# One tile of gathered rows in 64 moves from GpSimd's indirect transfers to 128 single transfers of SP

## What is computed

```python
src, dst = (edge_index[0], edge_index[1])
s_e = s[src]                      # gathered scalars, 8 of the 32 numbers of a row
v_e = v[src]                      # gathered vectors, 24 of the 32
...
out0 = jax.ops.segment_sum(m0, dst, num_segments=n)
out1 = jax.ops.segment_sum(m1.reshape(e, MUL * 3), dst, num_segments=n).reshape(n, MUL, 3)
```

## Time and profile before

| | |
|---|---|
| Median of 3 runs | 4191.23 us (4188.38 to 4191.39) |
| The profiled execution | 4180.82 us, span of its instructions 4179.0 us |
| Busy share | PE 86%, PEld 52%, DVE 79%, ACT 53%, POOL 72% |
| Layer 0, first to last gather | from 26.4 to 2036.7 us |
| Layer 1, first to last gather | from 2100.2 to 4108.0 us |

### The profile page before, as it was taken

How to read it: one execution, slowest core, us unless ns; L and a number is a source line. 1 busy time by engine, 2 the same in 40 slices (tenths; PEclk the granted TensorE clock), 3 DMA queues, 4 the chain that set the end, 5 groups by cost and what they waited for, 6 DMA issues and landing times.

```text
span 4179.0 us, 79599 instructions
## 1 busy us (share of the span) xinstructions
PE 3584.4 (86%) x24746; PEld 2173.1 (52%) x24746; DVE 3311.0 (79%) x5246; ACT 2201.5 (53%) x6573; POOL 3017.6 (72%) x3143
## 2 busy tenths in 40 slices
PE   5888888888888888888649999999999999999995
PEld 3555555555555555555425555555555555555553
DVE  7777777777777777777749988888888889888887
ACT  3555555555555555555325555555555556555553
POOL 5777777777777777777367777777777777777772
PEclk8999999999999999999879999999999999999998
DMA  3111111111111111111132212121212212121212
GB/s 103 33 29 33 29 33 29 34 33 29 33 29 33 29 33 29 33 31 31 18 48 47 46 39 47 37 47 37 47 37 47 47 37 48 37 47 37 47 37 32
DMA packets 220966, 159.83 MB, mean 38 GB/s; under 512 B 125489, under 2 KB 194994, under 8 KB 220466
## 3 DMA queue, kind: packets, MB, share of 16 engines
q0 software_dynamic: 100352, 51.58, 8.8%
q1 hardware_dynamic: 84946, 90.16, 8.2%
q10 hardware_dynamic: 35650, 17.88, 1.6%
HBM read 148.94 MB, written 10.43 MB: 38 GB/s over the span
## 4 chain that ended last, share of the span: by engine, by line
POOL 58%; issue 25%; PE 7%; DVE 6%; DMA 3%; DVEq 1%; POOLq 0%; ACT 0%; SPq 0%; ACTq 0%
POOL rows L364 58%; PE red L687 4%; PE wps L674 2%; DMA rows<-x_rows,src 2%; DVE prod L984 1%; DVE q L1036 1%; DMA src<-in_src 1%; PE wps L667 1%; DVE t_a L1022 0%; DVEq L1064 0%; DVE table L1060 0%; POOLq L381 0%; DMA x_rows<-table 0%; PE acc L701 0%; DMA rows<-in_x,src 0%
## 5 line engine op out<-in xcount | busy, mean ns | idle before, releaser
L364 POOL DMA_INDIRECT rows<-x_rows,src x1568 | 1504.6, 960 | 567.2 <-issue 562.7
L364 POOL DMA_INDIRECT rows<-in_x,src x1568 | 1512.1, 964 | 507.9 <-issue 498.5
L687 PE MATMUL red<-prod,ident 128*128 128x336 f32 (+2 forms) x6272 | 1753.6, 436 | 0.0
L687 PEld LDWEIGHTS red<-prod,ident 128*128 128x128 f32 x6272 | 1145.9, 193 | 651.1 <-issue 189.5
L493 ACT ACTIVATE gap<-iota,slot_plan 128x128 bf16<-128x128 f32 x3136 | 943.7, 387 | 85.3 <-DVE t_b L1087 76.0
L984 DVE TENSOR_TENSOR prod<-wps,q 128x896 f32<-128x896 f32 x784 | 836.3, 1084 | 191.2 <-PE wps L674 175.9
L667 PE MATMUL wps<-bias_parts,ones 64*128 64x448 bf16 (+1 forms) x2352 | 463.6, 391 | 517.4 <-DVE prod L978 324.4
L674 PE MATMUL wps<-w_sb,hidden 64*128 64x256 f32 (+1 forms) x4704 | 903.8, 487 | 0.0
L511 ACT ACTIVATE sums<-red 128x336 f32<-128x336 f32 (+2 forms) x392 | 168.6, 430 | 1084.1 <-PE red L687 1083.1
L667 PEld LDWEIGHTS wps<-bias_parts,ones 64*128 64x128 bf16 x2352 | 114.5, 94 | 1039.6 <-DVE prod L978 422.1
L674 PEld LDWEIGHTS wps<-w_sb,hidden 64*128 64x128 f32 x4704 | 487.5, 204 | 70.4 <-issue 25.6
(11 more groups left out here) (125 smaller groups left out, 3117.4 us busy)
## 6 DMA issues: line engine op xcount, KB each, us to landing
mlp<-in_dist SPq DMA_DIRECT2D x196, 256.0 KB
mlp<-in_feat SPq DMA_DIRECT2D x98, 256.0 KB
rows<-in_x,src POOLq DMA_INDIRECT x1568
rows<-x_rows,src POOLq DMA_INDIRECT x1568
frames<-frame ACTq DMA_DIRECT2D x49, 144.0 KB
geo<-frames ACTq DMA_DIRECT2D x98, 72.0 KB
src<-in_src SPq DMA_DIRECT2D x196, 8.0 KB, 1.6
geo<-in_sh ACTq DMA_DIRECT2D x98, 32.0 KB, 1.7
```

Source lines behind the costliest of these rows:

```text
L364: nc.gpsimd.indirect_dma_start(out=rows[z][:, t, :], out_offset=None, in_=table_rows, in_offset=bass.IndirectOffsetOnAxis(ap=src_sb[z][:, ...
L687: ins = nc.tensor.matmul(red[:, bank * 512:bank * 512 + cols], ident[:], pr[:, i, :, a:b, :], start=(i == 0), stop=(i == MUL - 1))
```

## The change

Every fourth chunk has its last tile (tile 15) fetched by SP instead of POOL. Four chunks make one pass of a new loop on SP and on POOL (`FETCHES` = 24 passes), and the last two of the 98 chunks are done as before. In one pass SP

- loads the 128 indices of that tile into one partition, `fetch_index`;
- loads for each of the four chunks `src` and the network's input, in this order chunk by chunk, and after each fetches 32 rows: eight times it loads four indices into registers, and for each it issues a transfer of one row of the table into one partition of `fetched`;
- waits for all 128 rows, then for the buffer's old rows to be read, and stores `fetched` into tile 15 of `rows[1]` with one transfer from SBUF to SBUF;
- waits until that has landed (`tile_moved`) and turns.

POOL gathers 63 tiles in a pass and adds the missing 16 to `rows_gathered` with `inc_swdge_sem`. DVE and ACT wait for `tile_moved` too before they read the second buffer.

```diff
+FETCH_CHUNKS = 4
+FETCH_ROUNDS = FETCH_CHUNKS // RING
+FETCHES = ROUNDS // FETCH_ROUNDS
+FETCH_ROWS = P // FETCH_CHUNKS
...
+            def fetch_rows(n, part):
+
+                table_rows = x if n == 0 else x1
+                for p in range(part * FETCH_ROWS, (part + 1) * FETCH_ROWS, 4):
+                    _, indices = nc.values_load_multi_w_load_instructions(
+                        fetch_index[0:1, p:p + 4], engines=(mybir.EngineType.SP,), min_val=0, max_val=N_NODES - 1,
+                        skip_runtime_bounds_check_because="the indices of the edges' sources are rows of the table")
+                    for a, index in enumerate(indices):
+                        sp.dma_start(fetched[p + a:p + a + 1, :], table_rows[bass.ds(index, 1), :]
+                                     ).then_inc(row_fetched, 16)
...
+                    with sp.Fori(0, FETCHES) as h:
+                        f = sp.snap(j * FETCHES + h + 1 + n * (count * FETCHES))
+                        sp.dma_start(fetch_index[:], src_fetched[bass.ds(h, 1), :]).then_inc(indices_loaded, 16)
+                        sp.sem_inc(s.tile_moved, 16)
+                        for m in range(FETCH_CHUNKS):
+                            z = m % RING
+                            r = round_of(sp, j, h * FETCH_ROUNDS + m // RING)
+                            k = h * FETCH_CHUNKS + m
+                            load_source(n, z, r, k)
+                            load_mlp(n, z, r, k)
+                            if m == 0:
+                                sp.wait_ge(indices_loaded, f * 16)
+                                if n == 1:
+                                    sp.wait_ge(x1_stored, 16)
+                                sp.sem_inc(fetch_turns, 1)
+                            fetch_rows(n, m)
+                        sp.wait_ge(row_fetched, 16 * P)
+                        sp.sem_clear(row_fetched)
+                        sp.wait_ge(s.rows_read[RING - 1], r)
+                        sp.wait_ge(s.rows_copied[RING - 1], r)
+                        sp.dma_start(rows[RING - 1][:, TILES - 1, :], fetched[:]).then_inc(s.tile_moved, 16)
+                        sp.wait_ge(s.tile_moved, r * 16)
+                        sp.sem_inc(fetch_turns, 1)
+                    sp.sem_inc(s.tile_moved, 16)
+                    for z in range(RING):
+                        r = round_of(sp, j, ROUNDS - 1)
+                        load_source(n, z, r, (ROUNDS - 1) * RING + z)
+                        load_mlp(n, z, r, (ROUNDS - 1) * RING + z)
...
-                for t in range(TILES):
+                for t in range(tiles):
...
+                if tiles < TILES:
+                    pool.inc_swdge_sem([s.rows_gathered[z]], [(TILES - tiles) * 16], mode="add")
...
                 act.wait_ge(s.rows_gathered[z], i * (16 * TILES) + 16 * TILES)
+                if z == RING - 1:
+                    act.wait_ge(s.tile_moved, r * 16)
...
                 dve.wait_ge(s.rows_gathered[z], i * (16 * TILES) + 16 * TILES)
+                if z == RING - 1:
+                    dve.wait_ge(s.tile_moved, r * 16)
```

More of the change, by code:

```diff
@@ L85, in build @@
 def build(nc, x, x_nodes, x_self, src, dst, dst_rows, sh, feat, rel, dist, identity, w1_0, b1_0, w2_0, si, w1_1, b1_1,
-          w2_1, out):
+          w2_1, src_fetched, out):
     x1 = nc.dram_tensor("x1_rows", [BLOCKS * P, FEAT], F32).ap()
@@ L140, in build @@
         span = sb("span", [P, 4])
+        fetch_index = sb("fetch_index", [1, P], I32)
+        fetched = sb("fetched", [P, FEAT])
         span_max = sb("span_max", [P, 2])
@@ L201, in build @@
         windows_moved = sem("windows_moved")
+        indices_loaded = sem("indices_loaded")
+        row_fetched = sem("row_fetched")
+        fetch_turns = sem("fetch_turns")
         class LayerSemaphores:
@@ L219, in __init__ @@
                 self.counts_reset = sem(f"l{n}_counts_reset")
+                self.tile_moved = sem(f"l{n}_tile_moved")
                 self.rows_read = ring("rows_read")
@@ L307, in _, with load_source, load_mlp @@
             sp.dma_start(rel_sb[:], rel).then_inc(loaded["rel"], 16)
+            def load_source(n, z, r, k):
+                s = layers[n]
+                sp.wait_ge(s.rows_read[z], r)
+                sp.dma_start(src_sb[z][:], src[bass.ds(k, 1)].rearrange("k p t -> p (k t)")
+                             ).then_inc(s.src_loaded[z], 16)
+            def load_mlp(n, z, r, k):
+                s = layers[n]
+                if n == 0:
+                    sp.wait_ge(s.hidden_summed[z], r * 2)
+                    sp.dma_start(mlp_sb[z][:, 0:SET], feat[bass.ds(k, 1)].rearrange("k p c -> p (k c)")
+                                 ).then_inc(s.mlp_loaded[z], 16)
+                else:
+                    sp.wait_ge(s.hidden_ready[z], r * 2)
+                    for a in range(2):
+                        sp.dma_start(mlp_sb[z][a * HID:(a + 1) * HID, :],
+                                     dist[bass.ds(k, 1), a, :].broadcast_to([HID, CHUNK // 2])
+                                     ).then_inc(s.mlp_loaded[z], 16)
+            def fetch_rows(n, part):
[7 more added lines that the diff above has]
+                                     ).then_inc(row_fetched, 16)
             def stream(n, count):
@@ L311, in stream @@
                 with sp.Fori(0, count) as j:
[L312 to L329, removed]
@@ L353, in _, with gather @@
                                            bass.bass_isa.ReduceOp.max).then_inc(spans_known, 1)
-            def gather(n, z, r):
+            def gather(n, z, r, tiles=TILES):
                 s = layers[n]
@@ L380, in gather_all @@
                 with pool.Fori(0, count) as j:
[L381 to L384, removed]
+                    with pool.Fori(0, FETCHES) as h:
+                        for m in range(FETCH_CHUNKS):
+                            gather(n, m % RING, round_of(pool, j, h * FETCH_ROUNDS + m // RING),
+                                   TILES - (1 if m == FETCH_CHUNKS - 1 else 0))
+                    for z in range(RING):
+                        gather(n, z, round_of(pool, j, ROUNDS - 1))
                     reset_counts(n, round_of(pool, j, ROUNDS - 1))
@@ L1328 @@
         "src": by_partition(padded(src, EDGES, 0)),
+        "src_fetched": padded(src, EDGES, 0).reshape(CHUNKS, TILES, P)[FETCH_CHUNKS - 1:FETCHES * FETCH_CHUNKS:FETCH_CHUNKS,
+                                                                       TILES - 1],
         "dst": all_by_partition(dst_p),
```

## The result

The changed kernel takes **4403.49 us** in the median of 4 runs (4399.19 to 4409.05), the kernel before on the same chip 4191.31 (4188.38 to 4195.27). The ratio is 1.0506, with an interval of 1.0492 to 1.0521: slower by 5.1%. The prediction was 4390 us.

A forecast was written before the change was run, and what follows sets the result against it. POOL's gathers were taken to bound the kernel before, at 82.0 and 81.8 us for four chunks. SP's summed passes of 84.6 and 87.5 us add 199 us, giving a median of 4390 us, range 4140 to 4750.

The forecast's parts named there:

- The bound: SP becomes the slowest, at 84.6 and 87.5 us a pass against POOL's 82.0 and 81.8 before: +199 us.
- The single transfer: SP's one-row fetch: 0.485 us from one to the next, 128 a pass, 62.1 us; bounds 0.47 and 0.68.
- rival 1: POOL stays the bound and the removed gathers count: SP's pass at 81.0 us, kernel 4142 us, chance 0.15.
- The register load: SP's load of four indices: 0.30 us plus 0.075 for gaps, 32 a pass, 12.0 us; bounds 0.29 and 0.47.
- rival 2: SP's small terms at upper bounds, a register load at 0.47 us: kernel 4650 us, up to 4750, chance 0.17.
- The code: SP's longer loop may fetch its code anew each turn: 2.0 us a pass taken, 0 and 5.6 kept.
- The ends of a pass: SP's waits: 1.3 us for the last row, 1.7 for the store into `rows`, 0.3 for semaphores.
- Rival 3: SP's single transfers are dear, at 0.492 us each: kernel 5590 us, or over twice the time if serial; chance 0.13.

The follow-up runs named there:

- e1: The changed kernel without SP's single-row transfers and register loads, tile 15 of every fourth chunk filled with zeros: 4094.42 us, 0.9778 of the kernel before.
- e3: The changed kernel with sixteen indices in one register load instead of four, 8 loads a pass instead of 32: 4095.95 us, 0.978 of the kernel before.
- e8: The changed kernel with register loads of sixteen indices and the back-branch prefetch hint on SP's loop together: 4096.22 us, 0.9792 of the kernel before.
- e4: The changed kernel with a prefetch hint for the back branch of SP's loop: 4246.39 us, 1.0139 of the kernel before.
- e12: The changed kernel with two indices in one register load instead of four, on another chip: 8022.11 us against 6875.8 for the kernel before.

## Why the prediction was right

**The bound.** Predicted: SP becomes the slowest at 84.6 us a pass in layer 0 and 87.5 in layer 1. Measured: 84.87 and 89.49. The difference between the layers is 4.6 us instead of 2.9. The sum of 24 x (84.87 - 82.0) + 24 x (89.49 - 81.8) is 253 us, against the predicted 199. The profiled execution was longer than that of before by 228 us, and the medians lie 212 apart. Some 8 us of the gap between them are the first index load of layer 1, which lasted 7.904 us: it is in the mean of the passes, but lies ahead of the layer's first gather. I have not followed the rest. e1, e3 and e8 show that it is SP's pass and nothing else: with the fetch gone or made shorter the loss is gone. So the mechanism is right: SP's pass as the bound, and POOL, DVE and ACT behind it.

**The single transfer.** Predicted 0.485 us, 62.1 a pass. From the records' starts the three instructions and their gaps take 55.6 us, 0.434 each. In them is the 1.0 us of waiting for the last row, which the prediction counts by itself, so 54.6 stand against the 62.1. The register instruction and the MOVE are 37 and 29 ns (50 and 29 priced). The issue lasts 0.228 us, under the 0.296 of L406 on ACT, from which I took the lower bound. The pitch of 0.47 was thus no bound. With all else as summed this pitch would have been rival 1, whose line was 0.445.

**The register load.** Predicted 0.375 us with its gap, 12.0 a pass. Measured 18.45 us in layer 0 and 20.2 in layer 1, 0.58 to 0.63 each. That is more than the upper bound, rival 2's 0.47 and its gap of 0.075. On this term rival 2 was right, and beyond its own price. The two loads on SP and DVE that I read as "a first one is dearer" were, at 0.470 and 0.556, nearer to it than DVE's 0.344 in its loop. The floor of about 600 ns in the Trainium skill, "DMA: Bandwidth & Descriptors", under "Latency and other measured facts", is near the measured 0.555 on SP. By it my sum for layer 0 would have been 84.6 + 9.6 = 94.2 us as an estimate, 9.3 too long, mostly since the transfers were too dear as well. The trace comes near the page for SP at four values. DVE's loads (0.344) lie well below that floor. The 1.227 us for sixteen values do not contradict a floor, but its figure would be half of the price there.

**The two errors cancel, and that is luck.** -7.5 us for the transfers and +6.4 for the loads, with the smaller terms, leave layer 0 within 0.3 us. The prediction's number is better than its terms, and its direction hung on them: with the transfers as measured and the loads as I had them, the sums would have been 77.1 and about 80 us, below POOL's, and the kernel faster, as in e3. With the loads alone as measured they would have given about 4740 us, near the upper end of the range.

**The code.** Predicted 2.0 us a pass, without a row. e4 measured 2.9 and 4.1. The 261 packets of 8 KB more than before are 5.4 for each of the 48 passes; I had asked for new packets of 16 KB. Without the code the sums were 82.6 and 85.5 us, and e4's passes 82.01 and 85.41.

**The ends of a pass.** The last rows land 1.0 us after their issue is done (1.3 predicted). Issue and landing of the store are 0.51 and 1.4 us (1.7 predicted). No wait for the index load shows, as counted.

**Rival 1 was priced wrong.** It had POOL alone giving 49 us. e1 and e3 gave 94 and 93. Of it 60 us are the 48 gathers at 1.25 us, since the increment costs nothing beside them. Some 39 us are the 2 us stops, less what is left of them. Longer gathers, 71 us over 0.944 in e3 against 56 in before, take about 15 back. These sum to the 84 us by which the gathers of the two traces differ. The medians lie 93 apart, since the traced run of the kernel before, on another chip, was shorter than the runs beside e3. The step that failed there is the reading of the earlier trace rows, where I called the excess "0.03 us above the pitch because some gathers are longer". Only about half of it was that (56 us over 3136 gathers). The other half was the stops. A mean over a window hides whether its excess is many small delays or a few stops.

**Rival 3** is out by the row of L348: 0.228 us, and the landings overlap. A cost of the counts that the prediction has the issuing sequencer write is not seen either: this is the shortest issue of all.

## What to carry to other kernels

When work moves to an idle queue, add up its whole pass, small instructions and landings included, and set it against the pass of the engine that it relieves. Here the same change is 5.1% slower or 2.2% faster (4403 or 4096 us, e3, with e8 the fastest of the kernels that compute everything) by the number of values in a register load alone. Price each instruction by a row of the same engine in the same form, and treat a lone row as a guess, not as a bound. Before a mean pace is taken for the bound's pace, look at its longest gaps: a regular stop is worth finding, since a change may shorten it by accident.

## What the runs showed of the hardware

- A transfer of one 128-byte row with its address in a register takes SP 0.228 us to issue, and 0.434 from one to the next with its two register instructions. A 128-partition one takes 0.333.
- A register load on SP lasts 0.555 us for four values, 1.227 for sixteen, and 0.728 for two on another chip, where no other count was run (e12). DVE's of four lasts 0.344.
- A loop of 457 to 465 instructions on SP fetches its code anew at each turn: 5.4 packets of 8 KB and 2.9 to 4.1 us a pass, with stops 128 instructions apart. A hint for the back branch brings the packets from 271 to 17 in e4, and to 134 in e8. At what length of the loop this begins was not measured.
- POOL's semaphore increment is recorded with 0.39 to 1.96 us in the changed kernel and costs the gathers nothing.
- POOL stops every seventh chunk of a layer, with 16 gathers in each chunk for 2 us behind the first gather of it. It does so with any number of chunks in its loop's turn, with increments between, and with gathers ahead. With 63 in four chunks the stops come every 110 or 111 gathers, behind the second or third of a chunk, shorter, or too short to be seen. Where they come from stays open. A run with 65 on a chip where POOL is the bound would have told more.
